# Round one of a two-round graph and state-space kernel: features of two row tiles in one group of VectorE operations, one tile later

## The chip, the cores and the metric

One Trainium2 chip, one core. The time is the device time of one execution in microseconds, and the median of several executions is taken. The profile is one further execution, recorded by the hardware profiler; its span runs from the first to the last instruction.

## The reference

`x` has 4096 rows of 128 features, `adj` is a 4096 x 4096 matrix of 0 and 1. The part that matters here is the graph layer on the normalised x:

```python
e = leaky_relu(x @ a[:F] + (x @ a[F:]).T, 0.2)
U = softmax(where(adj > 0, e, -9e15), axis=1)
prop_u = (0.5 * U) @ x
rowsum = sum(U * 0.5 * U, axis=1)
xi = x * rowsum[:, None]
feat = coe[2] * (prop_u - xi) + (1 - coe[2]) * (x + prop_u - xi)
feat = where(abs(feat) > 1e-6, abs(feat) - 1e-6, 0) * sign(feat)
pu = U @ feat
```

`pu`, `feat` and `h0` are then combined, x is added, and a layer with a gated state-space scan (convolution, softplus, scan over 32 chunks, gate, normalisation, output matrix) follows on the normalised sum.

## The kernel before

The 4096 rows are 32 row tiles of 128. The kernel goes over all of them twice, since `U @ feat` needs every tile's `feat`. **Round one** computes `U @ x` and `rowsum`, and from them each tile's `feat`, which is written over the tile's rows in `xn`. **Round two** computes `U @ feat` and, a few tiles behind, the state-space layer.

Round one runs in 8 supertiles of 4 row tiles (`it` 0 to 3), and each row tile in 4 blocks (`ch` 0 to 3), so 16 blocks b per supertile. The adjacency never takes part as numbers. For supertile G+1, ScalarE (ACT) turns adjacency words into 16-bit `edges` (`sign`, line 1208), TensorE (PE) transposes them (`turn`, line 1550, into one of 4 banks), and VectorE (DVE) compares them with the scores and writes one-byte `code` (`codes`, line 762, two per block). For supertile G, ACT makes `maskA` and DVE makes `maskC` from the code (lines 1271 and 770), two blocks ahead (`LEAD`), in 4 buffers each. PE multiplies both with `Y` (`products`, lines 1609 and 1618): 8 matmuls into `accA`, 8 into `accC`, in one of two banks by the row tile's parity.

There is no scheduler. Every engine runs its own instruction order, which is written out by hand (`supertile` for each of them), and semaphores tie them. Supertile 0 and supertile 7 are written out, and supertiles 1 to 6 are a hardware loop of two. The waits around the change:

- PE, in block b: `products(b)`, then `turn(G+1, b)`. Before the first block of tile T+2, PE waits for ACT's and DVE's reading of tile T's sums (`free_acc`, `acc_read` and `summed`).
- ACT reads tile T's `accA` during block 1 of tile T+1 (`read_acc`).
- DVE, in block b: the mask of block b+2; `codes(G+1, ...)` twice, which wait for PE's turn of block b (`tr_done`); in block 2 also `sum1` of the tile before (line 787), which adds `accC` and counts `summed`. Behind it comes the feature step `feat1` of the tile before that.
- GpSimd (POOL) computes from `ps_sum` the small numbers of a tile and `scaled` and `k_one` (`features`, lines 526 to 545, in a chain of dependent operations). It begins when `summed` says so and counts `scaled_done`. It has two sets of these buffers, by parity, and waits for `feat_done` before it overwrites one. For odd tiles it also adds two finished tiles of `xn` to `featsum` (`feature_sum`, line 551).
- `feat1` waits for `scaled_done`. Its three dependent operations (lines 796 to 798) form the feature, limit it to plus or minus 1e-6, and subtract the two. The last one writes `xn` and counts `feat_done`.

In the last supertile there are no codes to make. Instead ACT and DVE prepare `Y2`, the operand of round two, from finished features (`y2_high`, `y2_low`, lines 1266 and 749, in the order of the table `Y2_AT`). Tiles 30 and 31 have a tail of their own (lines 905 to 931), in which both tiles' limit and subtraction are one operation each.

Of the kernel before, what the change touches and what calls it, by code (L numbers as in the profile page):

```python
# [25 lines left out]
ALU = mybir.AluOpType  # L26
# [5 lines left out]
THRESH = 1e-06  # L32
# [7 lines left out]
def gnn_ffn_kernel(nc, x, adj, h0, a, temp, W_in, conv_w, conv_b, dt_bias, A_log, D, norm_w, W_out, W_lin, b_lin, out):  # L40
    N, F = x.shape
    NT = N // P
    IT = 4
# [19 lines left out]
    with ExitStack() as ctx:  # L63
        def sb(name, shape, dt=F32):
            return ctx.enter_context(nc.sbuf_tensor(name, shape, dt))

        def sem(name):
            return ctx.enter_context(nc.semaphore(name))
# [20 lines left out]
        xn = sb("xn", [P, NT, F])  # L89
# [32 lines left out]
        k_one = sb("k_one", [P, 2, 1])  # L122
# [4 lines left out]
        scaled = sb("scaled", [P, 2, F])  # L127
        fwork = sb("fwork", [P, 2, F])
# [110 lines left out]
        S = {n: sem(n) for n in names}  # L239
# [6 lines left out]
        def wait(eng, name, value):  # L246

            if not isinstance(value, int) or value > 0:
                eng.wait_ge(S[name], value)
# [438 lines left out]
        def _(dve):  # L688
            v = nc.vector
# [54 lines left out]
            def y2_low(t):  # L744

                for side in range(2):
                    dve.wait_ge(S["y2_hi"], 2 * t + side + 1)
                    y = y2_of(t, side)
                    v.scalar_tensor_tensor(out=y[:, 1], in0=xn[:, t, :], scalar=colw[:, side, t, 0:1], in1=y[:, 0].bitcast(F32),
                                           op0=ALU.mult, op1=ALU.subtract).then_inc(S["y2_done"], 1)  # L750
# [6 lines left out]
            def codes(G, par, jt):  # L757

                n = G * NT + jt
                dve.wait_ge(S["tr_done"], n + 1)  # L760
                rows = bass.ds(v.snap(G * 512) if not isinstance(G, int) else G * 512, 512)
                v.scalar_tensor_tensor(  # L762
                    out=code[par][:, :, jt * P:(jt + 1) * P], in0=f1_rows[:, rows].rearrange("p (i r) -> p i r", i=IT),
                    scalar=neg_f2[:, jt:jt + 1], in1=turned(jt),
                    op0=ALU.is_le, op1=ALU.subtract).then_inc(S["coded"], 1)
# [6 lines left out]
            def mask1(G, par, b):  # L772

                if b >= BLOCKS:
                    G, par, b = G + 1, 1 - par, b - BLOCKS
                it, ch = b // NB, b % NB
                dve.wait_ge(S["coded"], G * NT + (NT if it else (ch + 1) * JB))
                mask_c(G * BLOCKS + b, code[par][:, it, ch * JB * P:(ch + 1) * JB * P], b)

            def sum1(T, k):  # L780

                row = v.snap(T) if not isinstance(T, int) else T
                w = roww[:, bass.ds(row, 1), 1:2].rearrange("p a b -> p (a b)")
                dve.wait_ge(S["acc_read"], T + 1)
                wait(dve, "scaled_done", T - 1)
                both = accC[k][:, 0:2 * XC].rearrange("p (a b) -> p a b", a=2)
                v.scalar_tensor_tensor(out=ps_sum[:, k], in0=both, scalar=w, in1=acc_s[:, k], op0=ALU.mult, op1=ALU.add).then_inc(S["summed"], 1)  # L787

            def feat1(T, k):

                row = v.snap(T) if not isinstance(T, int) else T
                mine = xn[:, bass.ds(row, 1), :].rearrange("p a b -> p (a b)")
                wait(dve, "feat_done", T)
                dve.wait_ge(S["scaled_done"], T + 1)
                inside = chain[0] > 0
                link(v.scalar_tensor_tensor(out=fwork[:, 0], in0=mine, scalar=k_one[:, k], in1=scaled[:, k], op0=ALU.mult, op1=ALU.add))
                link(v.tensor_scalar(fwork[:, 1], fwork[:, 0], -THRESH, THRESH, ALU.max, ALU.min))
                v.tensor_tensor(mine, fwork[:, 0], fwork[:, 1], ALU.subtract).then_inc(S["feat_done"], 1)
                if inside:
                    dve.wait_ge(S["feat_done"], T + 1)  # L800
                else:
                    end_chain()

            def supertile(G, par, first=False, last=False):
                for b in range(BLOCKS):
                    it, ch = b // NB, b % NB
                    if not (last and b + LEAD >= BLOCKS):
                        mask1(G, par, b + LEAD)
                    if not last:
                        if b == 0:  # L810

                            wait(dve, "maskA_ready", G * BLOCKS)
                            wait(dve, "spilled", G * IT * 16)
                        if first and b == 0:
                            dve.wait_ge(S["f1_copied"], 8)
                            dve.wait_ge(S["yC_done"], NB)
                            dve.wait_ge(S["yA_done"], NB)
                        for j in range(JH):
                            codes(G + 1, 1 - par, b * JH + j)
                    if ch == 2 and not (first and it < 1):  # L820
                        sum1(G * IT + (it - 1), (it - 1) % 2)
                    if ch == 2 and not (first and it < 2):
                        feat1(G * IT + (it - 2), it % 2)

            chain = [0]

            def step(ins):

                chain[0] += 1
                ins.then_inc(S["vch"], 1)  # L830
                return chain[0]

            def link(ins):

                dve.wait_ge(S["vch"], step(ins))

            def end_chain():
                if chain[0]:
                    dve.wait_ge(S["vch"], chain[0])
                    v.sem_clear(S["vch"])  # L840
                chain[0] = 0
# [29 lines left out]
            def mask2(n, k, j):  # L871

                b = j % NB
                if isinstance(n, int) and n < 2 * NB:

                    T, ch = FIRST[n]
                    dve.wait_ge(S[f"codes_in{T}"], 16)
                    mask_c(n + R1, code0[:, T, ch * JB * P:(ch + 1) * JB * P], b)
                    return
                dve.wait_ge(S[f"codes_in{k}"], code_count(n, k, b))  # L880
                mask_c(n + R1, code0[:, k, b * JB * P:(b + 1) * JB * P], b)

            G = NG - 1
            for b in range(BLOCKS):
                it, ch = b // NB, b % NB
                if b + LEAD < BLOCKS:
                    mask1(G, 1, b + LEAD)
                else:
                    mask2(b + LEAD - BLOCKS, 0, b + LEAD - BLOCKS)
                if ch == (1 if it == IT - 1 else 2):  # L890
                    sum1(G * IT + (it - 1), (it - 1) % 2)
                if ch == 2 and it < IT - 1:
                    feat1(G * IT + (it - 2), it % 2)
                for t in Y2_AT[b]:
                    y2_low(t)

# [26 lines left out]
            for i in range(2):  # L923
                made = step(v.tensor_scalar(fwork[:, i], xn[:, NT - 2 + i, :], k_T[:, i:i + 1], None, ALU.mult))
            dve.wait_ge(S["vch"], made)
            for i in range(2):
                made = step(v.scalar_tensor_tensor(out=fwork[:, i], in0=scaled[:, i], scalar=r_T[:, i:i + 1], in1=fwork[:, i], op0=ALU.mult, op1=ALU.add))
# [268 lines left out]
        def _(act):  # L1196
# [192 lines left out]
            def read_inputs(c, kc):  # L1389
                zdt, _, conv, _ = in_buffers(c)  # L1390
                first, second = in_banks(c)
                own = isinstance(c, int) and c == LAST
                act.wait_ge(S["p_in"], c + 1)
                if not own:
                    wait(act, "dt_ready", c)
                    wait(act, "gate_done", c)
                s.copy(zdt, first[:, 0:DI + NH]).then_inc(S["zcopy"], 1)  # L1397
                wait(act, "conv_pre", c - 1)
                s.copy(hist[:, kc, :, TAPS - 1:], second[:, 0:CB * P].rearrange("p (c w) -> p c w", c=CB))
                if not own:  # L1400
                    wait(act, "conv_ready", c)
                for cb in range(CB):
                    m = s.activation(conv[:, cb], second[:, cb * P:(cb + 1) * P], ACT.Identity, bias=conv_bt[:, cb:cb + 1],  # L1403
                                     scale=conv_wt[:, cb, TAPS - 1:TAPS])
                m.then_inc(S["in_read"], 1)
                if not own:

                    act.wait_ge(S["in_read"], c + 1)
                    wait(act, "conv_pre", c)
                    s.copy(hist[:, 1 - kc, :, 0:TAPS - 1], hist[:, kc, :, P:P + TAPS - 1]).then_inc(S["halo_done"], 1)  # L1410
# [474 lines left out]
```

## Time and profile before

| | |
|---|---|
| median of 3 executions | 808.99 us (808.49 to 809.42) |
| profiled execution | 808.94 us |
| its span | 807.2 us |
| TensorE busy | 756.7 us, 94% |
| VectorE busy | 739.7 us, 92% |
| ScalarE busy | 675.4 us, 84% |
| GpSimd busy | 582.9 us, 72% |
| round one, about | from 47 to 351 us |

A busy time counts the instructions of an engine, not its waiting for semaphores, so the difference from the span is what an engine idles. PE has two lines in the profile: PE for matmuls and PEld for the weight loads that run beside them. Because matmuls are pipelined, a weight load's start tells better than a matmul's when a block began. In the order of time, a start is followed by a duration; a DVE operation's successor can start before its duration is over, so what an operation costs in a row of others is the distance of two starts.

### The profile page before, as it was taken

To read this page: it belongs to the slowest core of one execution; us is meant where nothing else is said; L and a number is where in the kernel's file an instruction comes from. 1 tells how busy PE (TensorE), PEld (TensorE's weight loads), DVE (VectorE), ACT (ScalarE), POOL (GpSimd) and SP (SyncE) were. 2 spreads that over 40 slices of the span, in tenths; PEclk is the share of its full clock that TensorE was granted. 3 is DMA by queue.
4 is the path that set the end of the run, shared out by engine and by line. 5 is a ranking of instruction groups with operands and counts; after the bars stand their busy time and mean duration, and the time that the engine had idled before them with its cause. 6 is when DMAs were issued, how large, how long until landed. Compare 5 with 4: busy or idle time off the path is not lost. (4 is left out here: it accounts for less than half of the span.)

```text
span 807.2 us, 20951 instructions
## 1 busy us (share of the span) xinstructions
PE 756.7 (94%) x6079; PEld 721.4 (89%) x6079; DVE 739.7 (92%) x1934; ACT 675.4 (84%) x1428; POOL 582.9 (72%) x1115
## 2 busy tenths in 40 slices
PE   3689999999999999869999999999999999999976
PEld 1389999999999999868899999999999999999955
DVE  6999999999999999796999999999999999999872
ACT  5989898989989897865888888888898989888761
POOL 5683667776777677856888878788787878788850
PEclk9989999999999999979999999999999999999975
DMA  7689897989889794122111121112121212110000
GB/s 212 191 257 328 267 326 242 336 259 325 273 302 291 258 308 184 29 53 81 56 55 66 44 67 44 65 42 68 42 69 39 68 39 68 46 37 14 5 8 10
DMA packets 97961, 110.43 MB, mean 137 GB/s; under 512 B 6865, under 2 KB 89713, under 8 KB 97905
## 3 DMA queue, kind: packets, MB, share of 16 engines
q1 hardware_dynamic: 97906, 109.78, 41.9%
q8 instruction: 25, 0.41, 0.2%
q14 instruction: 30, 0.25, 0.1%
HBM read 90.87 MB, written 18.89 MB: 136 GB/s over the span
## 5 line engine op out<-in xcount | busy, mean ns | idle before, releaser
L1271 ACT ACTIVATE maskA<-code 128x1024 fp32r<-128x1024 int8 x256 | 269.0, 1053 | 24.9 <-DVE code L762 21.4
L1609 PE MATMUL accA<-Y,maskA 128*128 128x260 f32 (+1 forms) x1792 | 270.6, 294 | 8.9 <-ACT maskA L1271 6.1
L1618 PE MATMUL accC<-Y,maskC 128*128 128x260 f32 (+1 forms) x1792 | 254.6, 285 | 2.6 <-DVE maskC L770 2.6
L1609 PEld LDWEIGHTS accA<-Y,maskA 128*128 128x128 f32 x1792 | 232.6, 191 | 14.4 <-issue 7.8
L1618 PEld LDWEIGHTS accC<-Y,maskC 128*128 128x128 f32 x1792 | 230.6, 191 | 3.6 <-DVE maskC L770 3.6
L770 DVE TENSOR_SCALAR maskC<-code 128x1024 fp32r<-128x1024 int8 x256 | 206.5, 808 | 0.0
L762 DVE SCALAR_TENSOR_TENSOR code<-f_rows,neg_f,ps 128x512 int8<-128x512 int8 (+1 forms) x256 | 177.9, 737 | 0.4 <-DVE neg_f L726 0.2
L1208 ACT ACTIVATE edges<-adj_in 128x1024 int8<-128x1024 f32 x128 | 135.2, 1059 | 1.5 <-DMA adj_in<-in_adj_dram 1.5
L625 POOL TENSOR_TENSOR room_r<-room,room_r 128x256 fp32r<-128x256 f32 x128 | 95.6, 774 | 2.5
L1044 DVE SCALAR_TENSOR_TENSOR room<-room 128x128 f32<-128x128 f32 x279 | 89.5, 342 | 0.0
L1550 PE MATMUL ps<-ident,edges 128*128 128x128 bf16 x512 | 51.2, 224 | 10.2 <-ACT edges L1208 10.2
L1550 PEld LDWEIGHTS ps<-ident,edges 128*128 128x128 bf16 x512 | 30.0, 99 | 20.2 <-ACT edges L1208 11.0
L613 POOL TENSOR_TENSOR room<-room,consts 128x1 f32<-128x1 f32 x32 | 8.7, 272 | 44.2 <-DVE room L1006 44.2
L526 POOL COPY small<-roww 128x2 f32 (+1 forms) x30 | 5.8, 194 | 47.7 <-DVE ps_sum L787 46.2
L1609 PE MATMUL accA<-Y_2a,maskA 128*128 128x256 f32 x256 | 38.0, 290 | 0.0
L1397 ACT COPY room<-ps 128x260 f32<-128x260 f32 x30 | 11.3, 378 | 30.9 <-PE ps L1700 30.9
L1716 PE MATMUL ps<-room 128*128 128x64 f32 x248 | 36.1, 270 | 0.0
L1618 PE MATMUL accC<-Y_2b,maskC 128*128 128x256 f32 x256 | 35.9, 283 | 0.0
L1403 ACT ACTIVATE room<-ps,room 128x128 f32<-128x128 f32 x90 | 35.3, 476 | 0.0
L1716 PEld LDWEIGHTS ps<-room 128*128 128x128 f32 x248 | 34.4, 201 | 0.0
L1452 ACT ACTIVATE room<-room 128x64 f32<-128x64 f32 x124 | 33.2, 343 | 0.0
L1618 PEld LDWEIGHTS accC<-Y_2b,maskC 128*128 128x128 f32 x256 | 32.9, 191 | 0.0
(260 smaller groups left out, 1620.9 us busy)
## 6 DMA issues: line engine op xcount, KB each, us to landing
adj_in<-in_adj_dram SPq DMA_DIRECT2D x128, 512.0 KB, 5.0
edge_codes<-code SPq DMA_DIRECT2D x32, 512.0 KB, 5.5
code<-edge_codes SPq DMA_DIRECT2D x32, 512.0 KB, 3.2
xn<-in_x_dram SPq DMA_DIRECT2D x4, 512.0 KB, 5.6
room<-in_x_dram SPq DMA_DIRECT2D x32, 64.0 KB, 1.8
room<-in_L_gnn_h_dram SPq DMA_DIRECT2D x32, 64.0 KB, 1.9
out_dram<-room SPq DMA_DIRECT2D x32, 64.0 KB, 1.6
room<-in_L_ffn_W_in_dram SPq DMA_DIRECT2D x1, 192.0 KB, 2.5
```

The source lines that it names most:

```text
L625: m = g.tensor_tensor(dam.rearrange("p a h w -> p (a h) w")[:, at], upto.unsqueeze(1).broadcast_to([P, NH // 2, P]), da_parts.rearrange("p ...
L762: v.scalar_tensor_tensor(out=code[par][:, :, jt * P:(jt + 1) * P], in0=f1_rows[:, rows].rearrange("p (i r) -> p i r", i=IT), scalar=neg_f2 ...
L770: v.tensor_scalar(maskC[:, b % MASKS], src, 1.0 - LINK, None, ALU.is_equal).then_inc(S["maskC_ready"], 1)
L1044: ins = v.scalar_tensor_tensor(out=conv[:, cb], in0=hist[:, kc, cb, tap:tap + P], scalar=conv_wt[:, cb, tap:tap + 1], in1=conv[:, cb], op0 ...
L1208: s.activation(pair, adj_in[:, h % 4].rearrange("p i (e w) -> p i e w", e=JH), ACT.Relu, bias=FREE, scale=HUGE).then_inc(S["signed"], 1)
L1271: s.activation(maskA[:, b % MASKS], src, ACT.Relu, bias=1.0 - LINK, scale=-1.0).then_inc(S["maskA_ready"], 1)
L1403: m = s.activation(conv[:, cb], second[:, cb * P:(cb + 1) * P], ACT.Identity, bias=conv_bt[:, cb:cb + 1], scale=conv_wt[:, cb, TAPS - 1:TAPS])
L1452: last = s.activation(xdtd[:, h * HD:(h + 1) * HD], xdt[:, h * HD:(h + 1) * HD], ACT.Copy, scale=expD[:, h, P - 1:P])
L1550: m = t_.matmul(ps[b % TRB][:, it * P:(it + 1) * P], edges[:, b % EDGE_SLOTS, it], ident2[:], start=True, stop=True)
L1609: t_.matmul(accA[k][:, 0:2 * cols], maskA[:, b % MASKS, l * P:(l + 1) * P], y2_of(jt, 0) if cols == F else Y[:, jt, 0, :, 0:cols], start=j ...
L1618: m = t_.matmul(accC[k][:, 0:2 * cols], maskC[:, b % MASKS, l * P:(l + 1) * P], y2_of(jt, 1) if cols == F else Y[:, jt, 1, :, 0:cols], sta ...
L1716: t_.matmul(ps[0][:, h * HD:(h + 1) * HD], mix_of(c)[:, h], xdt[:, h * HD:(h + 1) * HD], start=False, stop=h == (kb + 1) * P // HD - 1)
```

## The change

A new function treats tiles T and T+1 (T even) together. Two operations form the features, one per tile, without a wait between them. One operation limits both, one subtracts both and counts `feat_done` by 2. It stands where the second tile's `feat1` stood, so the first tile's feature comes one tile later. The limited values go to `scaled`, as in the tail of tiles 30 and 31. Tiles 28 and 29 keep their single `feat1`.

```diff
+            def feat_pair(T):
+
+                row = v.snap(T) if not isinstance(T, int) else T
+                both = xn[:, bass.ds(row, 2), :]
+                wait(dve, "feat_done", T)
+                for i in range(2):
+                    dve.wait_ge(S["scaled_done"], T + 1 + i)
+                    mine = xn[:, bass.ds(v.snap(T + i) if not isinstance(T, int) else T + i, 1), :].rearrange("p a b -> p (a b)")
+                    made = step(v.scalar_tensor_tensor(out=fwork[:, i], in0=mine, scalar=k_one[:, i], in1=scaled[:, i], op0=ALU.mult, op1=ALU.add))
+                dve.wait_ge(S["vch"], made)
+                link(v.tensor_scalar(scaled[:], fwork[:], -THRESH, THRESH, ALU.max, ALU.min))
+                v.tensor_tensor(both, fwork[:], scaled[:], ALU.subtract).then_inc(S["feat_done"], 2)
+                end_chain()
...
-                    if ch == 2 and not (first and it < 2):
-                        feat1(G * IT + (it - 2), it % 2)
+                    if ch == 2 and it % 2 == 1 and not (first and it < 2):
+                        feat_pair(G * IT + (it - 3))
...
-                if ch == 2 and it < IT - 1:
-                    feat1(G * IT + (it - 2), it % 2)
+                if ch == 2 and it == 1:
+                    feat_pair(G * IT - 2)
+                if ch == 2 and it == 2:
+                    feat1(G * IT, 0)
```

DVE's order in block 2 of row tile 2 (it = 2 of supertile 0, from the `sum1` of tile 1 on). Line 787 is `sum1`, 796 to 798 are `feat1`, 840 clears the counter of dependent operations, 770 is the mask and 762 the codes. Before:

```order
L787 SCALAR_TENSOR_TENSOR ps_sum<-accC,roww,acc_s 128x260 [waits acc_read]
L796 SCALAR_TENSOR_TENSOR fwork<-xn,k_one,scaled 128x128 [waits scaled_done]
L797 TENSOR_SCALAR fwork<-fwork 128x128 [waits vch]
L798 TENSOR_TENSOR xn<-fwork 128x128 [waits vch]
L840 ISA [waits vch]
L770 TENSOR_SCALAR maskC<-code 128x1024 [waits mm_done,coded]
L762 SCALAR_TENSOR_TENSOR code<-f_rows,neg_f,ps 128x4x128 [waits tr_done] x2
```

And now, at the same place:

```order
L787 SCALAR_TENSOR_TENSOR ps_sum<-accC,roww,acc_s 128x260 [waits acc_read]
L770 TENSOR_SCALAR maskC<-code 128x1024 [waits mm_done,coded]
L762 SCALAR_TENSOR_TENSOR code<-f_rows,neg_f,ps 128x4x128 [waits tr_done] x2
L770 TENSOR_SCALAR maskC<-code 128x1024 [waits mm_done,coded]
L762 SCALAR_TENSOR_TENSOR code<-f_rows,neg_f,ps 128x4x128 [waits tr_done] x2
```

The feature step is gone from behind this `sum1`, and the next mask follows it at once. The same holds for every `sum1` of an odd tile in the loop.

DVE's order one tile later (it = 3, from the `sum1` of tile 2 on). In the new numbering, 812 to 815 are `feat_pair` and 854 is the clearing. Before:

```order
L787 SCALAR_TENSOR_TENSOR ps_sum<-accC,roww,acc_s 128x260 [waits scaled_done,acc_read]
L796 SCALAR_TENSOR_TENSOR fwork<-xn,k_one,scaled 128x128 [waits scaled_done,feat_done]
L797 TENSOR_SCALAR fwork<-fwork 128x128 [waits vch]
L798 TENSOR_TENSOR xn<-fwork 128x128 [waits vch]
L840 ISA [waits vch]
L770 TENSOR_SCALAR maskC<-code 128x1024 [waits mm_done,coded]
```

And now:

```order
L787 SCALAR_TENSOR_TENSOR ps_sum<-accC,roww,acc_s 128x260 [waits scaled_done,acc_read]
L812 SCALAR_TENSOR_TENSOR fwork<-xn,k_one,scaled 128x128 [waits scaled_done] x2
L814 TENSOR_SCALAR scaled<-fwork 128x256 [waits vch]
L815 TENSOR_TENSOR xn<-fwork,scaled 128x256 [waits vch]
L854 ISA [waits vch]
L770 TENSOR_SCALAR maskC<-code 128x1024 [waits mm_done,coded]
```

The step of one tile has become that of two, with four operations for six. The order of PE, ACT, POOL and the DMA queue is the same in both kernels.

## Rows read from the trace of the kernel before

**Rows 1.** The page: busy time and share of the span of each engine.
```profile
PE 756.7 (94%) x6079; PEld 721.4 (89%) x6079; DVE 739.7 (92%) x1934; ACT 675.4 (84%) x1428; POOL 582.9 (72%) x1115
```

**Rows 2.** Table by stretch: length, then busy us of PE, PEld, DVE, ACT, POOL.
```profile
200.24:209.35 9.11, 9.11 (x84) 8.90 (x84) 9.04 (x17) 6.31 (x9) 5.95 (x14) 1.00 0.68 224
209.35:218.28 8.93, 8.89 (x81) 8.55 (x80) 8.86 (x18) 8.93 (x12) 6.77 (x15) 1.00 0.88 289
```

**Rows 3.** Order of time, 200 to 219 us: start, duration, engine, line, operation.
```profile
200.24 0.48 DVE L787 SCALAR_TENSOR_TENSOR ps_sum<-accC,roww,acc_s 128x260 f32<-128x260 f32 x1
200.64 0.34 DVE L796 SCALAR_TENSOR_TENSOR fwork<-xn,k_one,scaled 128x128 f32<-128x128 f32 x1
...
201.50 0.68 DVE L770 TENSOR_SCALAR maskC<-code 128x1024 fp32r<-128x1024 int8 x1
...
202.10 1.39 DVE L762 SCALAR_TENSOR_TENSOR code<-f_rows,neg_f,ps 128x512 int8<-128x512 int8 x2
...
203.42 0.68 DVE L770 TENSOR_SCALAR maskC<-code 128x1024 fp32r<-128x1024 int8 x1
...
207.16 0.40 POOL L544 TENSOR_TENSOR scaled<-featw,small 128x128 f32<-128x128 f32 x1
207.25 0.86 DVE L770 TENSOR_SCALAR maskC<-code 128x1024 fp32r<-128x1024 int8 x1
...
207.29 0.40 PE L1550 MATMUL ps<-ident,edges 128*128 128x128 bf16 x4
...
208.03 1.39 DVE L762 SCALAR_TENSOR_TENSOR code<-f_rows,neg_f,ps 128x512 int8<-128x512 int8 x2
...
209.35 0.48 DVE L787 SCALAR_TENSOR_TENSOR ps_sum<-accC,roww,acc_s 128x260 f32<-128x260 f32 x1
...
209.90 1.03 PEld L1609 LDWEIGHTS accA<-Y,maskA 128*128 128x128 f32 x8 [0.18 <-issue]
...
218.83 1.03 PEld L1609 LDWEIGHTS accA<-Y,maskA 128*128 128x128 f32 x8
```

**Rows 4.** Order of time in supertile 0, 79 to 93 us, around tiles 1 and 2.
```profile
79.27 1.41 DVE L762 SCALAR_TENSOR_TENSOR code<-f_rows,neg_f,ps 128x512 int8<-128x512 f32 x2 [0.20 <-PE ps L1550]
...
81.04 0.40 PE L1550 MATMUL ps<-ident,edges 128*128 128x128 bf16 x4
...
81.48 1.41 DVE L762 SCALAR_TENSOR_TENSOR code<-f_rows,neg_f,ps 128x512 int8<-128x512 f32 x2
...
83.25 0.40 PE L1550 MATMUL ps<-ident,edges 128*128 128x128 bf16 x4
83.43 1.02 PEld L1609 LDWEIGHTS accA<-Y,maskA 128*128 128x128 f32 x8
...
91.95 0.48 DVE L787 SCALAR_TENSOR_TENSOR ps_sum<-accC,roww,acc_s 128x260 f32<-128x260 f32 x1
...
92.67 0.42 PEld L1609 LDWEIGHTS accA<-Y,maskA 128*128 128x128 f32 x3 [0.37 <-issue]
```

**Rows 5.** Order of time on DVE in the tail, tiles 30 and 31.
```profile
356.00 0.61 DVE L927 SCALAR_TENSOR_TENSOR fwork<-scaled,row_out,fwork 128x128 f32<-128x128 f32 x2
356.65 0.29 DVE L929 TENSOR_SCALAR scaled<-fwork 128x256 f32<-128x256 f32 x1
356.97 0.43 DVE L930 TENSOR_TENSOR xn<-fwork,scaled 128x256 f32<-128x256 f32 x1
357.32 2.54 DVE L749 SCALAR_TENSOR_TENSOR Y<-xn,colw,Y 128x128 fp32r<-128x128 f32 x8
```

**Rows 6.** Order of time on PEld: the gate behind tile 26's `sum1`.
```profile
309.08 1.02 PEld L1609 LDWEIGHTS accA<-Y,maskA 128*128 128x128 f32 x8
```

**Rows 7.** Who waited for whom, 308 to 360 us: us in total, times, longest.
```profile
DVE fwork L796 <- POOLq L457: 6.6, 3, 2.9
...
PE accC L1618 <- DVE maskC L770: 2.3, 3, 1.3
POOL small L526 <- POOL row_out L545: 1.5, 3, 0.7
```

## The prediction

> **What bounds the kernel now.** I read the page's first part, then a table of busy time by stretch, then the order of time around one row tile. The page has TensorE (PE) busy for 94% of the span and VectorE (DVE) for 92% [rows 1]. The table by stretch has both at 99 to 100% in a tile of round one [rows 2]. So shares do not say who waits. The order of time does [rows 3]. PE's first weight load of a tile's first block (call it the gate) comes at 209.90 and at 218.83. The first is 0.07 us behind the end of a `sum1` on DVE (209.35 + 0.48 = 209.83). A block of PE takes 2.21 us (two turns without a wait between them, 81.04 and 83.25, [rows 4]), so four take 8.83 us, but these gates are 8.93 us apart, and those from 92.67 to 309.08, over 24 tiles, 9.02 us on average [rows 4, 6]. PE therefore waits about 0.2 us per tile for DVE, and DVE never rests: **DVE sets the pace by the last step of a short loop**. The loop is this: `codes(b)` waits for PE's turn of block b, `sum1` stands behind the codes of block 2, and PE's gate of the tile after next waits for `sum1`.
>
> How far may DVE run ahead? Hardly at all. In block 2 the codes start at 208.03, and PE's turn of the same block ended at 207.29 + 0.40 = 207.69 [rows 3]: 0.34 us of room. One tile of the trace has no feature step behind its `sum1`, the first one, and shows what happens with less work on DVE: codes start at 79.27 with idle time put down to PE's turn, then at 81.48, one PE block later and 0.04 us behind the end of the turn of 81.04 [rows 4]. There DVE runs at PE's pace, its spare time is lost, and the gate comes at 83.43, 0.18 us behind the turn, which is PE's unhindered distance.
>
> **The change part by part.** For tiles 0 to 27 the six feature instructions of two tiles become four, 14 times. They all stand behind the `sum1` of an even tile; the `sum1` of an odd tile is followed by the next mask.
>
> DVE's work. Going by starts, a mask holds DVE for 0.60 us (201.50 to 202.10), two codes for 1.32 (202.10 to 203.42), a `sum1` for 0.40 (200.24 to 200.64) and a single feature step for 0.86 (200.64 to 201.50) [rows 3]. A tile is 4 x 1.92 + 0.40 = 8.08 us without a feature and 8.94 with one; the interval of 8.93 from 209.35 to 218.28 [rows 2] agrees. The pair's price is to be had from the tail of round one, where tiles 30 and 31 are treated in the same way [rows 5]: 0.65 us for two SCALAR_TENSOR_TENSOR (356.00 to 356.65), 0.32 for the limit over 256 elements, 0.35 for the subtraction, 1.32 us in all. So DVE is saved 2 x 0.86 - 1.32 = 0.40 us per pair. That is 14 x 0.40 = 5.6 us if all of it were on the path.
>
> It is not, because the work is now uneven: 8.08 us in one tile, 9.40 in the next. **Light interval** (from the gate behind an odd tile's `sum1` to that behind an even tile's): DVE needs 8.08 us, PE 8.83. DVE is held by the turns, as in [rows 4], and the gates are 8.83 apart. **Heavy interval**: at its start DVE has no lead. Its codes start 1.95 us ahead of the gate (81.48 and 83.43, [rows 4]). 9.40 us later the next codes of block 2 start, `sum1` ends 1.32 + 0.48 = 1.80 us after that, and the gate opens 0.07 us later [rows 3] or 0.24 (91.95 + 0.48 = 92.43, gate 92.67, [rows 4]); both distances come back in runs of tiles, and I take the middle, 0.15. That makes 9.40 - 1.95 + 1.80 + 0.15 = 9.40 us.
>
> To it comes one collision. In the interval from 200.24 the mask at 207.25 took 0.86 us instead of 0.68 while POOL's `scaled` operation ran from 207.16 [rows 3]; the next interval has none, and 9.11 against 8.93 us is this difference [rows 2]. It falls behind the `sum1` of an even tile, which is where the heavy interval lies. Its price is bounded from below by 0 (the four-tile pattern of starts moves by 0.46 us and may miss it) and from above by two such collisions, 0.36; I take 0.18, since the work of POOL that starts with an even tile's `sum1` stays the same. The heavy interval is then 9.58 us. A test of the method: the same sum with a feature of 0.86, the late gate of 0.24 and 0.18 gives 8.94 - 1.95 + 1.80 + 0.24 + 0.18 = 9.21; the trace has 92.67 - 83.43 = 9.24 [rows 4], after just such a light interval.
>
> The Trainium skill, page "SBUF — State Buffer", section "Who interferes with whom", calls this an exclusive lock between VectorE and GpSimd, and adds that a VectorE operation with two SBUF inputs takes part in it too. By that, the pair's 256-element subtraction may collide as well, and the sum would go to the upper bound; the row of 356.97 shows it undisturbed, with no such neighbour named there.
>
> Sum. A light and a heavy interval take 8.83 + 9.58 = 18.41 us; now 24 intervals from 92.67 to 309.08 are 12 pairs of 18.03. 12 x 0.38 = +4.6 us. The interval from 83.43 to 92.67 loses the feature step behind tile 1's `sum1` and becomes light: 8.83 - 9.24 = -0.4. In the last supertile there are no codes, and what paces it is POOL: DVE waits 6.6 us in three waits for its `scaled`, and POOL goes from one tile's operations to the next with 0.7 us or less between [rows 7]. This chain starts at tile 26's `sum1`, which will end about 0.15 us ahead of its gate instead of 0.06: -0.1. The feature of tile 26, for which DVE waits there, moves one tile on; POOL hides what this saves. The pair that takes its place adds 0.46 us to a tile in which PE already waits for maskC (2.3 us in three waits, [rows 7]); I cost it at nothing, since POOL's chain is longer, and at 0.5 if it were not. `feature_sum` on POOL asks for both features of an older pair and finds them done. Round two gets nothing new. **+4.6 - 0.4 - 0.1 = +4.1 us.** The profiled execution took 808.94, 0.05 below the median of the runs: 813.0.
>
> **The rivals.** Two tenths of a per cent, 1.6 us, is about what a measurement can tell here.
>
> *DVE keeps its lead* (0.07). If the time saved in a light interval could be carried over, the pair of tiles would be DVE's 18.03 - 0.40 = 17.63, or PE's floor of 17.66. That is 12 x 0.37 + 0.4 = 4.8 us less: 804.1, faster. It decides at the codes of block 2: they would have to start more than 0.5 us ahead of where the turn now lets them. For it speaks that two instructions in six vanish; against it the rows of the first tile.
>
> The Trainium skill, page "VectorE: DVE Perf Modes", section on the TRN2 errata, has a fixed cost of 58 cycles at 0.96 GHz for each instruction that reads SBUF. As an estimate from that page, 28 fewer instructions are 1.7 us, which gives 807.2 if DVE is the path throughout. The rows give more for the merging and deny that it is the path throughout.
>
> *Two collisions in a heavy interval* (0.17). 9.76 instead of 9.58, 12 x 0.18 = 2.2 us more: 815.2. For it: masks now start 0.46 us later against the fourteen operations that POOL issues for a tile, any of which can stand in the way. With the late gate of 0.24 throughout as well it is 816.3.
>
> *No collision* (0.11). 2.2 us less than forecast: 810.8; with the early gate of 0.07 throughout, 809.9, which counts as no change. I give half of this case to either.
>
> *The change does not reach the end* (0.04), since something I have not seen, DMA or ScalarE, paces the tiles and refills what moves: 808.9. The gates' distance of 0.07 to 0.24 us from `sum1` speaks against it.
>
> *POOL is late for the pair* (0.01): the odd tile's `scaled` is now needed at the second instruction. The single step needed it at the same place, so the price is small.
>
> **How the numbers follow.** My forecast has 0.60. Slower: 0.60 + 0.17 + 0.06 + 0.01 = 0.84. Within 0.2%: 0.05 + 0.04 = 0.09. Faster: 0.07. The range leaves out the faster rival, the case of no effect and the outer ends: 810.3 to 815.8.
>
> **What would show it.** In the profile after, intervals between gates should alternate at 8.8 and 9.5 to 9.6 us. DVE should show idle time, or masks and codes drawn out, behind PE's turns in tiles that have no pair. The pair's operations should take 0.34, 0.34, 0.29 and 0.43 us. DVE's busy time for features should fall by some 5 us and the span grow by 4. Intervals of 8.83 throughout would make it wrong, and so would codes that start before the turn of their block has ended by my reading.

## The result, and the profile after

The changed kernel takes 813.39 us in the median of 5 executions (810.08 to 814.42), the kernel before 808.49 in its 5 of the same comparison. The ratio is 1.0063, with a 95% interval of 1.0041 to 1.0085: **slower by 0.6%, some 5 us**. A second series of the same kernel, told of below, has 813.46 against 809.05, ratio 1.0059 [1.0036, 1.0083].

The page of the kernel after, busy time by engine, answers to [rows 1]:

```profile
PE 750.9 (93%) x6079; PEld 716.5 (89%) x6079; DVE 739.8 (92%) x1906; ACT 675.5 (84%) x1428; POOL 595.0 (74%) x1115
```

DVE has 28 instructions fewer, and the durations of its feature instructions add up to 4.7 us less. Yet its busy time has not moved, since it counts time that two instructions cover only once: in an unhindered row each starts a little before the last has ended (a mask of 0.68 us is followed after 0.60), and where DVE is held this overlap is gone. The groups of DVE by shape show the part of the holding that the profile calls idle. The columns are line, engine, operation and shapes, count, busy us and mean ns, and then idle us before them with what ended it. Before:

```profile
L762 DVE SCALAR_TENSOR_TENSOR code<-f_rows,neg_f,ps 128x512 int8<-128x512 int8 x192 | 133.9, 736 | 0.0
```

After:

```profile
L762 DVE SCALAR_TENSOR_TENSOR code<-f_rows,neg_f,ps 128x512 int8<-128x512 int8 x192 | 134.3, 740 | 5.8 <-PE ps L1566 5.8
L812 DVE SCALAR_TENSOR_TENSOR fwork<-xn,k_one,scaled 128x128 f32<-128x128 f32 x28 | 8.6, 344 | 2.8 <-POOLq L457 2.8
L815 DVE TENSOR_TENSOR xn<-fwork,scaled 128x256 f32 x12 | 5.1, 425 | 1.2
L814 DVE TENSOR_SCALAR scaled<-fwork 128x256 f32<-128x256 f32 x14 | 4.1, 295 | 0.5
```

Before, the codes never idled; now DVE idles 5.8 us ahead of them, all of it put down to PE's turn (line 1566 in the new numbering). More of the wait lies inside instructions: the codes of 220.15 below start 0.88 us behind their mask of 219.27, where 0.60 is the unhindered distance, and the profile calls 0.20 of this 0.28 idle.

Table by stretch of the kernel after, the intervals between `sum1` of tiles 14, 15 and 16 (length, then busy us of PE, PEld, DVE, ACT, POOL). It answers to [rows 2]:

```profile
203.03:212.71 9.68, 9.67 (x90) 9.23 (x88) 9.54 (x18) 6.38 (x9) 6.91 (x16) 1.00 0.66 212
212.71:221.47 8.76, 8.18 (x73) 8.06 (x74) 8.33 (x14) 8.76 (x12) 6.86 (x14) 1.00 0.88 288
```

What was 9.11 and 8.93 is now 9.68 and 8.76. Order of time of the kernel after, the same stretch, answers to [rows 3]. Lines 1566 and 1625 are PE's turn and first product.

```profile
203.03 0.48 DVE L787 SCALAR_TENSOR_TENSOR ps_sum<-accC,roww,acc_s 128x260 f32<-128x260 f32 x1
203.43 0.61 DVE L812 SCALAR_TENSOR_TENSOR fwork<-xn,k_one,scaled 128x128 f32<-128x128 f32 x2
203.66 1.02 PEld L1625 LDWEIGHTS accA<-Y,maskA 128*128 128x128 f32 x8
204.07 0.29 DVE L814 TENSOR_SCALAR scaled<-fwork 128x256 f32<-128x256 f32 x1
204.07 0.33 POOL L526 COPY small<-roww 128x2 f32 x1 [0.67 <-DVE ps_sum L787]
204.47 0.43 DVE L815 TENSOR_TENSOR xn<-fwork,scaled 128x256 f32 x1
204.81 0.69 DVE L770 TENSOR_SCALAR maskC<-code 128x1024 fp32r<-128x1024 int8 x1
...
210.46 0.46 POOL L543 TENSOR_TENSOR featw<-featw,num 128x128 f32<-128x128 f32 x1
210.57 0.91 DVE L770 TENSOR_SCALAR maskC<-code 128x1024 fp32r<-128x1024 int8 x1
...
211.40 1.39 DVE L762 SCALAR_TENSOR_TENSOR code<-f_rows,neg_f,ps 128x512 int8<-128x512 int8 x2
...
212.71 0.47 DVE L787 SCALAR_TENSOR_TENSOR ps_sum<-accC,roww,acc_s 128x260 f32<-128x260 f32 x1
...
213.26 1.02 PEld L1625 LDWEIGHTS accA<-Y,maskA 128*128 128x128 f32 x8 [0.73 <-issue]
...
219.27 0.68 DVE L770 TENSOR_SCALAR maskC<-code 128x1024 fp32r<-128x1024 int8 x1
219.72 0.40 PE L1566 MATMUL ps<-ident,edges 128*128 128x128 bf16 x4
...
220.15 1.41 DVE L762 SCALAR_TENSOR_TENSOR code<-f_rows,neg_f,ps 128x512 int8<-128x512 int8 x2 [0.20 <-PE ps L1566]
...
221.47 0.48 DVE L787 SCALAR_TENSOR_TENSOR ps_sum<-accC,roww,acc_s 128x260 f32<-128x260 f32 x1
...
222.10 1.02 PEld L1625 LDWEIGHTS accA<-Y,maskA 128*128 128x128 f32 x8
```

The gates are at 203.66, 213.26 and 222.10: 9.60 us for the heavy interval, in which PE waits 0.7 us for `sum1`, and 8.84 for the light one. At the end of the light one, the codes (220.15) start 0.03 us behind the end of PE's turn (219.72 + 0.40). This is the picture of [rows 4], now in every second tile. Over the 12 pairs from tile 2 to tile 26, light intervals are 8.82 to 8.93 us (mean 8.87), heavy ones 9.59 to 9.68 (9.64), 18.50 together instead of 18.03.

By the end of round one (the gate behind tile 31's `sum1`), the kernel after is 5.3 us behind: 356.52 against 351.23. Yet the span of its first profile is only 1.2 us longer, 808.4. The last update of x1 in round two begins 5.1 us later than before (769.9 against 764.8), so the 3.9 us come back in the drain behind it. The tables of this stretch show the clock (the third number from the right). Before:

```profile
764.00:780.00 16.00, 12.87 (x68) 11.29 (x68) 14.65 (x54) 9.57 (x34) 8.56 (x18) 0.77 0.02 6
780.00:808.00 28.00, 17.49 (x70) 14.59 (x68) 8.10 (x23) 7.24 (x28) 6.53 (x13) 0.62 0.03 10
```

After:

```profile
764.00:780.00 16.00, 12.46 (x94) 11.25 (x93) 12.99 (x44) 12.82 (x45) 10.20 (x23) 1.00 0.02 6
780.00:808.00 28.00, 18.09 (x87) 14.86 (x86) 13.46 (x42) 8.72 (x34) 9.42 (x18) 0.70 0.03 10
```

Here the granted clock of TensorE was 0.77 and 0.62 of its upper level (2.4 GHz) before, and 1.00 and 0.70 after. The stretches are fixed in time while the drain begins 5.1 us later, so a part of the first difference is only the shift. The rest, 0.70 against 0.62, is a difference between two executions, as the next section shows.

### The profile page after: what moved, and what is told of

It is laid out like the page before. It is cut to its first block and busy times, and to the rows that moved or that the text cites. A ratio compares the mean times of both kernels' runs of the same rounds, so it can differ in the third digit from the quotient of the medians.

```text
span 808.4 us, 20909 instructions
## 1 busy us (share of the span) xinstructions
PE 750.9 (93%) x6079; PEld 716.5 (89%) x6079; DVE 739.8 (92%) x1906; ACT 675.5 (84%) x1428; POOL 595.0 (74%) x1115
## 5 line engine op out<-in xcount | busy, mean ns | idle before, releaser
L526 POOL COPY small<-roww 128x2 f32 (+1 forms) x30 | 11.2, 373 | 41.4 <-DVE ps_sum L787 39.9
```

## The experiments

**The same kernel again.**

> The changed kernel once more, for a second profile and more executions. The tile intervals should repeat to 0.02 us (8.87 and 9.64), the last tiles of round one should stand 5.1 to 5.5 us behind the kernel before, and the median should be 4 to 5.5 us above it. The first profile had a span only 1.2 us longer; if that lay in the clock of the drain at the end (mean granted clock 0.979 against 0.970), it does not repeat.

Measured: 813.46 us (811.94 to 815.68) against 809.05, ratio 1.0059 [1.0036, 1.0083]. All intervals repeat within 0.03 us, tile 31's gate is at 356.57, and the span is 812.2, 5.0 above the profile before. Its last x1 update begins at 771.1. Its drain had this clock:

```profile
764.00:780.00 16.00, 12.94 (x97) 11.66 (x95) 12.99 (x47) 12.13 (x42) 10.12 (x24) 1.00 0.01 5
780.00:808.00 28.00, 20.74 (x87) 17.77 (x86) 14.75 (x42) 9.05 (x36) 9.71 (x17) 0.62 0.02 6
```

It took 41 us from that update to the end, the first profile 38.5, the kernel before 42.4. The 5 us of round one repeat; what the drain gives back does not.

**The delay without the merging.**

```diff
-                        feat_pair(G * IT + (it - 3))
+                        feat1(G * IT + (it - 3), 0)
+                        feat1(G * IT + (it - 2), 1)
```

(and likewise in the last supertile)

> Both features of a pair stand one tile later, as in the change, but as two single steps of three operations each: the delay without the merging. Theory A (in the tile without features DVE is held by PE's turns and its spare time is lost; the tile with both features then pays all of it at the gate): the heavy interval grows by 2 x 0.86 - 1.32 = 0.40 us over that of the change, from 9.64 to about 10.04, the light one stays at 8.87; 12 x 0.40 = 4.8 us more than the change, so about 818 us, 1.2% above the kernel before. Theory B (the place does not matter, the merged operations over 256 elements are what costs, by their collisions with POOL): the old operations bring the old time back, about 808.5.

Measured: 820.88 us against 809.23, ratio 1.0141 [1.0121, 1.0161]. Order of time, the gates of tiles 14, 15 and 16:

```profile
206.81 1.02 PEld L1627 LDWEIGHTS accA<-Y,maskA 128*128 128x128 f32 x8
...
216.94 1.02 PEld L1627 LDWEIGHTS accA<-Y,maskA 128*128 128x128 f32 x8 [1.11 <-issue]
```

The heavy interval is 10.13 to 10.20 us from tile 7 on, the light one stays at 8.83 to 8.92. So the very operations of the kernel before, at another place, cost 11.6 us; theory B falls. The heavy interval grew by 0.53 instead of 0.40: the two single steps hold DVE for 2.14 us (206.58 to 208.72) instead of 1.72, where the pair took 1.38, and the long mask of the change is missing (0.76 - 0.23 = 0.53). The merging by itself gains some 7 us against this kernel; the delay takes more.

**`sum1` ahead of the mask and codes of its block**, on the change and on the kernel before.

```diff
+                    if ch == 2 and not (first and it < 1):
+                        sum1(G * IT + (it - 1), (it - 1) % 2)
                     if not (last and b + LEAD >= BLOCKS):
                         mask1(G, par, b + LEAD)
...
-                    if ch == 2 and not (first and it < 1):
-                        sum1(G * IT + (it - 1), (it - 1) % 2)
```

> The change, with sum1 moved to the head of block 2, ahead of the mask and the codes of that block (supertiles 0 to 6), so that PE's gate asks for it 1.9 us and more before it is due. Theory A: the gate no longer waits, the late work of a heavy tile is taken up by the room between sum1 and the gate, and DVE catches up in the light tile. A pair of intervals falls from 18.50 us to what DVE needs, 2 x 8.08 + 1.32 = 17.5 plus a collision or two, or PE's floor of 17.66, whichever is more: about 17.8. 12 x 0.7 = 8 us less than the change, so about 805, and below the kernel before. Theory B: DVE's work is the same and so is the time, about 813.

> The kernel before with sum1 at the head of block 2 in the same way. Theory A: here DVE has no time to spare in any tile (8.94 us of work each, PE 8.83), so an earlier sum1 cannot help: a pair stays at 2 x 8.94 + 0.18 = 18.06, time 808.5 within 1.5 us. If the wait at the gate cost by itself (its 0.07 to 0.24 us of latency, 24 times), it would fall by 2 to 5 us.

Measured: on the change 806.70 us against 809.23, ratio 0.9968 [0.9952, 0.9983]; on the kernel before 806.86, ratio 0.9974 [0.9955, 0.9992]. With the change, the loss is gone. Of its 6.7 us, 2.4 are what the same edit gives the kernel before, for a reason of its own (below); the other 4.3 are the time that the change had lost. The pair then neither costs nor gains: 806.70 and 806.86. The `sum1` of tiles 14, 15 and 16, on DVE:

```profile
196.85 0.48 DVE L787 SCALAR_TENSOR_TENSOR ps_sum<-accC,roww,acc_s 128x260 f32<-128x260 f32 x1
206.72 0.48 DVE L787 SCALAR_TENSOR_TENSOR ps_sum<-accC,roww,acc_s 128x260 f32<-128x260 f32 x1
214.94 0.48 DVE L787 SCALAR_TENSOR_TENSOR ps_sum<-accC,roww,acc_s 128x260 f32<-128x260 f32 x1
```

DVE now runs at its own pace, 9.87 + 8.22 = 18.09 us per pair. It no longer waits in light tiles (8.22 is below PE's 8.83), but 18.09 is 0.3 more than I expected, and no less than the 18.03 of the kernel before. DVE's bare work is 17.48. These lines of the heavy interval show what stretches it:

```profile
199.17 0.77 DVE L812 SCALAR_TENSOR_TENSOR fwork<-xn,k_one,scaled 128x128 f32<-128x128 f32 x2
...
200.74 0.69 DVE L770 TENSOR_SCALAR maskC<-code 128x1024 fp32r<-128x1024 int8 x1
...
204.47 0.46 POOL L543 TENSOR_TENSOR featw<-featw,num 128x128 f32<-128x128 f32 x1
204.57 0.91 DVE L770 TENSOR_SCALAR maskC<-code 128x1024 fp32r<-128x1024 int8 x1
```

The pair holds DVE for 1.57 us (199.17 to 200.74) instead of 1.32, one mask is 0.23 longer, and another, beside POOL's `featsum` operation, 0.14: 17.48 + 0.25 + 0.37 = 18.10.

On the kernel before, the intervals of `sum1` are unchanged (9.10 and 8.93), and yet it is 2.4 us faster, which my expectation put outside its bound. The gain is a single one: `sum1` stands 1.9 us earlier in the order, DVE is no longer held in the first tile, which has no feature step (8.07 instead of 8.75 us), and later tiles add hundredths. So POOL's chain for the last supertile starts at 306.21 instead of 309.19, and tile 31's gate comes 2.5 us earlier.

**PE's turn ahead of its block's products**, on both.

```diff
+                    if not last:
+                        turn(G + 1, b)
                     if ch == 0 and not (first and it < 2):
 
                         free_acc(G * IT + (it - 2))
                     products(G * BLOCKS + b, it % 2, b, ch, XC, 1 if first and it == 0 else None)
-                    if not last:
-                        turn(G + 1, b)
```

> The change, with PE's turn of a block ahead of the products of that block and ahead of the wait at the gate, instead of behind them: DVE's codes may start one PE block (2.2 us) earlier. sum1 stays where it was. Theory A: DVE keeps the time of the light tile as a lead and spends it in the heavy one: pair of intervals about 17.7 to 17.9 us, about 805 us. If DVE is not held by the turns (A wrong in that step), nothing changes: 813. Theory B: 813.

> The kernel before with PE's turn ahead of the products of its block. DVE has 8.94 us of work in each tile, more than PE's 8.83, so a lead gives it nothing to spend: pair of intervals 18.0 to 18.1 us. PE may get ahead once by some 1.5 to 2.5 us, as with the earlier sum1 (2.4 us faster): about 806.5 to 807.5. With the change on top the same edit gave 809.7, with pairs of 18.26 us on DVE; if that excess over 17.5 is collisions with POOL brought by the pair, here it should be absent.

Measured: on the change 809.72 us against 809.23, ratio 1.0009 [0.9991, 1.0027]; on the kernel before 808.06 against 809.05, ratio 0.9988 [0.9970, 1.0006]. DVE's hold by the turns is real: with it gone the change gets 3.7 us back (the kernel before, 1.0), and its light intervals fall to 8.22. But the pair is 10.04 + 8.22 = 18.26 us. Order of time at the feature step of this kernel:

```profile
218.01 0.47 DVE L787 SCALAR_TENSOR_TENSOR ps_sum<-accC,roww,acc_s 128x260 f32<-128x260 f32 x1
218.41 0.34 DVE L812 SCALAR_TENSOR_TENSOR fwork<-xn,k_one,scaled 128x128 f32<-128x128 f32 x1
218.49 0.30 POOL L545 COPY row_out<-small 128x4 f32 x1 [0.17 <-POOL scaled L544]
219.02 0.35 DVE L812 SCALAR_TENSOR_TENSOR fwork<-xn,k_one,scaled 128x128 f32<-128x128 f32 x1 [0.27 <-POOLq L457]
```

This is the rival to which I gave 0.01: once the light tile is short, POOL's work for the odd tile (over 8 us) is not ready when the pair asks for it. The second operation starts 0.61 us behind the first instead of 0.27. The kernel before shows no such thing with the same edit; its pair stays at 18.05.

**The pair split**: the even tile's operation one tile earlier.

```diff
+            def feat_open(T):
+
+                wait(dve, "feat_done", T)
+                dve.wait_ge(S["scaled_done"], T + 1)
...
+                step(v.scalar_tensor_tensor(out=fwork[:, 0], in0=mine, scalar=k_one[:, 0], in1=scaled[:, 0], op0=ALU.mult, op1=ALU.add))
+                end_chain()
...
+                    if ch == 2 and it % 2 == 0 and not (first and it < 2):
+                        feat_open(G * IT + (it - 2))
```

> The change with its first operation (the feature of the even tile, one SCALAR_TENSOR_TENSOR) done one tile earlier, behind the sum1 of the odd tile; the other three stay. It evens the two tiles out a little: about 0.3 us go from the heavy to the light one. Theory A (time is lost by unevenness, since DVE is held by PE's turns in the light tile and cannot work ahead): the light interval stays at 8.87, the heavy one falls from 9.64 to about 9.35; 12 x 0.3 = 3.5 us less than the change, about 809.5 to 810. Theory B (the merged operations cost by themselves): no change from 813.4, rather a bit more, for one more clearing of the counter per pair.

Measured: 816.78 us (814.03 to 819.01) against 809.05, ratio 1.0100 [1.0075, 1.0126]: not faster than the change, against my expectation. Its tile 26 gate is where the change has it (314.60 and 314.55). The reason is in the order of time:

```profile
221.50 0.19 POOL L545 COPY row_out<-small 128x4 f32 x1 [0.17 <-POOL scaled L544]
...
221.91 0.35 DVE L819 SCALAR_TENSOR_TENSOR fwork<-xn,k_one,scaled 128x128 f32<-128x128 f32 x1 [0.32 <-POOLq L457]
```

In the change, the first of the two operations fills just the time in which POOL finishes. Moved away, it leaves a wait of the same length. Of the further 3.3 us above the change, 1.2 lie in the last supertile (tile 31's gate at 357.74). Another 1.3 lie between tile 31's `sum1` and the last x1 update (416.7 us, 415.4 in the second profile of the change), where the granted clock was 0.91 from 370 to 390 us instead of 0.99. One profile does not show whether that belongs to the kernel.

**POOL shortened**, on the change, and then with the pair split. Both kernels leave out the part for rows without neighbours (the product of `col_mean` with their flag and its addition), which for these data adds zero.

```diff
-                link(g.tensor_tensor(featw[:, 0], col_mean[:], n["zn"].broadcast_to([P, F]), ALU.mult))
-                link(g.tensor_tensor(featw[:, 1], featw[:, 0], num[:, 0:F], ALU.add))
-                link(g.tensor_tensor(scaled[:, k], featw[:, 1], n["r"].broadcast_to([P, F]), ALU.mult))
+                link(g.tensor_tensor(scaled[:, k], num[:, 0:F], n["r"].broadcast_to([P, F]), ALU.mult))
```

> The change with two of POOL's fourteen operations per tile left out: the product of col_mean with the flag for an empty row and its addition to the sums (for these data the flag is 0 throughout). The mask at the end of the heavy interval then finds another operation of POOL, or none, beside it. Collision theory: in the change this mask takes 0.91 us instead of 0.68 since it starts while the addition runs; without it the heavy interval falls from 9.64 to 9.4 or 9.5, 12 x 0.15 to 0.24 = 2 to 3 us; in the last supertile POOL's chain of four tiles gets 4 x 0.95 us shorter, up to 3.8 us more: 807 to 810. If the long mask has another cause, the heavy interval stays and only the last supertile gains: 809.5 to 811.

> The split pair (first operation one tile earlier) with the two operations of POOL left out as in pool_short, so that POOL's result for the odd tile is there in time. In split_pair the second feature waited for POOL (0.3 us, starting 0.22 us behind POOL's last operation) and nothing was won. Theory A: with POOL in time, the heavy interval falls by about 0.3 us against pool_short, from 9.67 to about 9.35 (give or take one collision of 0.2), 12 x 0.3 = 3.5 us: about 807 against 810.3. If unevenness were not what costs, it would stay at 810.

Measured: shortened alone, 810.32 us against 809.05, ratio 1.0017 [1.0000, 1.0034]; with the split, 807.40 against 809.00, ratio 0.9986 [0.9973, 0.9998]. The first one's heavy interval did not fall, it is 9.60 to 9.70. The long mask is no longer at the end of the interval, but at its beginning, beside another wide operation of POOL:

```profile
207.44 0.67 POOL L529 TENSOR_TENSOR num<-ps_sum 128x130 f32<-128x130 f32 x1
207.75 0.91 DVE L768 TENSOR_SCALAR maskC<-code 128x1024 fp32r<-128x1024 int8 x1
```

So the long mask moved with POOL's operations, as a collision does, but it did not go away with the one that was removed. What this kernel gains over the change lies in the last supertile. With the split on top, POOL is in time, and now the evening out works as theory A has it. Gates of tiles 14, 15 and 16 of this kernel:

```profile
201.94 1.02 PEld L1634 LDWEIGHTS accA<-Y,maskA 128*128 128x128 f32 x8
...
211.28 1.03 PEld L1634 LDWEIGHTS accA<-Y,maskA 128*128 128x128 f32 x8 [0.47 <-issue]
...
220.13 1.02 PEld L1634 LDWEIGHTS accA<-Y,maskA 128*128 128x128 f32 x8
```

9.34 us (9.42 in the other tiles) against 9.62 (9.70), and 8.85: from tile 2 to 26, the pair falls from 18.52 to 18.24 us, 12 x 0.28 = 3.4 us; the medians differ by 2.9.

**Candidates for a faster kernel**: both early, then the pair one block later, then all three.

```diff
-                    if ch == 2 and it % 2 == 1 and not (first and it < 2):
+                    if ch == 3 and it % 2 == 1 and not (first and it < 2):
                         feat_pair(G * IT + (it - 3))
```

> The change with both edits that loosen PE and DVE: sum1 at the head of block 2, and PE's turn ahead of its block's products. Neither engine should then wait for the other more than once in a few tiles; the pace is DVE's own work. With sum1 early alone that was 18.09 us per pair, with collisions with POOL (24 long masks in 24 tiles, 0.2 us each) in it. If that is DVE's own pace, it stays at 18.1 and the time at 806 to 807. If the remaining waits of sum_early_after on turns (room 0.02 us in one tile in four) cost as well, it falls to 17.9 and 804.

> sum1 at the head of block 2, and the pair one block later, behind the codes of block 3, so that POOL's ten small operations meet other masks. A candidate for a kernel faster than both. DVE's bare work is 17.47 us per pair, PE's 17.66. Without long masks: 17.7 per pair, 18.09 - 17.7 = 0.4, 12 x 0.4 = 5 us less than sum_early_after, 802. If just as many collide as before: 806.7. POOL waits for the pair before it may write the next numbers; it comes there 4.6 us after sum1, the pair is done by then.

> sum1 at the head of block 2, PE's turn ahead of its products, and the pair behind the codes of block 3: the two candidates together. With sum1 early and the pair in block 3, DVE's pair of intervals was 17.8 us undisturbed, and PE waited for sum1 in some tiles only (intervals of 8.97 instead of 8.83). If the earlier turn takes these waits away too, the pair comes to 17.75 to 17.8 throughout, 0.15 to 0.2 less than the mean of 17.95 there, 12 x 0.15 = 2 us: 803.5. If DVE's own pace with its long masks is the limit in both, it stays at 805.5 to 806.5.

Measured: both early 806.45 us against 809.00, ratio 0.9958 [0.9940, 0.9977]; `sum1` early with the pair in block 3, 805.51, ratio 0.9966 [0.9951, 0.9981]; all three, **802.56 us against 809.01, ratio 0.9933 [0.9911, 0.9955]**. The first has 9.86 + 8.21 = 18.07 us per pair on DVE, as with `sum1` early alone: DVE's own pace is the limit. The second lies between its two forecasts of 802 and 806.7, with DVE at 17.91 us per pair in the mean. In the last one DVE has this, the `sum1` of tiles 15, 16 and 17 and the pair between:

```profile
204.00 0.47 DVE L787 SCALAR_TENSOR_TENSOR ps_sum<-accC,roww,acc_s 128x260 f32<-128x260 f32 x1
...
212.22 0.47 DVE L787 SCALAR_TENSOR_TENSOR ps_sum<-accC,roww,acc_s 128x260 f32<-128x260 f32 x1
...
216.46 0.60 DVE L812 SCALAR_TENSOR_TENSOR fwork<-xn,k_one,scaled 128x128 f32<-128x128 f32 x2
217.09 0.29 DVE L814 TENSOR_SCALAR scaled<-fwork 128x256 f32<-128x256 f32 x1
217.49 0.42 DVE L815 TENSOR_TENSOR xn<-fwork,scaled 128x256 f32 x1
...
221.81 0.48 DVE L787 SCALAR_TENSOR_TENSOR ps_sum<-accC,roww,acc_s 128x260 f32<-128x260 f32 x1
```

8.22 + 9.59 = 17.81 us per pair, with POOL's numbers long there when the pair comes; over all 12 pairs the mean is 17.91, as in the second kernel, and PE is nearly the slower one (17.66). Tile 31's gate is at 345.92, 5.3 us ahead of the kernel before.

How much of this is the merging? The fair comparison is with `sum1` early on the kernel before. Against it (806.86 us; 18.03 us per pair) the second candidate takes 274.42 us from tile 0's `sum1` to tile 31's instead of 275.79, 1.4 us less. The medians differ by as much, but the intervals of the two ratios overlap. The third takes 274.33 us there, hardly less than the second. These profiles do not explain why its median is 3 us lower than the second's, and both early edits without the merging were never run together. So of the 6.4 us, the traces show some 1.4 for the merging at its later place; how the rest divides is open.

## Why the prediction was right

The direction, the mechanism and the size held: 813.0 forecast, 813.39 measured. That the two agree to 0.4 us is luck in part. The trace's own terms add up to 5.6 - 0.3 - 0.2 = 5.1 us where the forecast had 4.1, and the medians differ by 4.9 and 4.4.

- *DVE sets the pace by the loop of codes, `sum1` and gate.* Held: in the change all gates but the undisturbed ones stand 0.07 to 0.24 us behind `sum1`; taking the loop apart at either of its ends (`sum1` early, turn early) recovers 6.7 and 3.7 us on the change, against 2.4 and 1.0 on the kernel before, whose intervals of `sum1` stay as they were, since DVE has nothing to spare there.
- *Saved time is lost in light tiles.* Held: at the end of every light interval the room at the codes of block 2 is 0.04 us, idle time ahead of the codes is 5.8 us where it was none. (The 0.34 us of room that I gave for the kernel before was that of one tile; its tiles have 0.06 to 0.41.)
- *The pair costs 1.32 us.* It took 1.38 (203.43 to 204.81): the limit holds DVE for 0.40 instead of 0.32. A collision with POOL's copy of 204.07 does not explain it: the distance is 0.40 to 0.42 in all 14 pairs, also where the copy was over long before (starts at 130.04 and 130.44, the copy ended at 130.05), and 0.40 in the last kernel above, where other operations of POOL are near. Why the tail has 0.32 is open. By the rule of the Trainium skill, page "SBUF — State Buffer", section "Who interferes with whom", the subtraction could have waited for POOL; no run shows that it did. The row of 356.97, which I had called undisturbed with no neighbour named, did have one: an operation of POOL over 128x30 from 356.86 to 357.10.
- *Light interval 8.83.* Measured 8.87: in half of the tiles PE still waits by 0.08 us, since the late gate's distance of 0.24 is more than the 0.15 by which `sum1` is early. The light interval that I had taken as a model was of the other kind.
- *Heavy interval 9.58.* Measured 9.64; the one collision is there, 0.23 us instead of 0.18.
- *12 pairs give +4.6.* They give 18.50 against 18.03, 5.6 us. The two steps above are the difference.
- *-0.4 for the interval behind tile 1.* It is 8.92 instead of 9.24: -0.3.
- *The last supertile hides its extra 0.46 us, and -0.1.* Held: the lag is 5.5 us at tile 26 and 5.3 at tile 31.
- *DVE's busy time for features falls by some 5 us.* Held, 4.7. Only in one sign did the first profile mislead: I had said that the span would grow by 4. It grew by 1.2, with a faster clock in the drain, and by 5.0 in the second.
- The rival "POOL is late" was dismissed too lightly. In the change POOL is in time by less than 0.1 us: its last operation before the pair ends at 203.41 (203.22 + 0.19), DVE in the other two kernels follows such an end by 0.22 us, and the second operation starts at about 203.70.

## What to carry to other kernels

Merging two steps of an engine that sets the pace saves its time only if the engine may run ahead during the lighter stretch. Look for the nearest thing that it waits for (here a transposition of the same block, 0.06 to 0.41 us away) before counting the saving, and for what stands behind the merged step in the order (here the small operation on which the next gate waits). Give it room first, by moving the released work earlier: that took away the 5 us that the pair had cost here. A gain from the merging itself, some 1.4 us in the traces, showed only when the pair had also been moved to where its inputs were long there. And run each such edit on the kernel without the change too: without the 2.4 us that `sum1` early gives the kernel before, one would credit the merging with a gain that it does not have.

## What the runs showed of the hardware

A mask of DVE takes 0.68 us alone. If it starts while POOL is in an operation over 128 elements or more, what counts is how long that operation still runs. With 0.31 us left it is 0.18 longer (207.25, kernel before), with 0.36 left 0.23 (210.57, the change), with 0.56 left 0.43 (once, `sum1` early on the change), always the time left less 0.13. With 0.11 left, nothing is added, nor where POOL's operation began only 0.01 us before the mask (then POOL's takes 0.95 instead of 0.40). The case with 0.11, in the kernel before:

```profile
216.07 0.40 POOL L542 TENSOR_TENSOR featw<-col_mean,small 128x128 f32<-128x128 f32 x1
216.36 0.69 DVE L770 TENSOR_SCALAR maskC<-code 128x1024 fp32r<-128x1024 int8 x1
```

So 24 of the 96 masks between the gates behind tiles 2 and 26 start beside such an operation in the kernel before, but only 12 are long: 0.2 us in the distance of two starts decides. In the change 12 of 96 are long too. Beside POOL's operations on one element (52 of the 84 short masks of the change) masks stay at 0.68 or 0.69. It is POOL that is drawn out there, 0.79 instead of 0.25 us for the operation at 206.66, although it began 0.07 us ahead of the mask. A wide operation that starts behind the mask is drawn out too (0.73 instead of 0.40 us for `scaled` at 211.00 in the kernel after). The Trainium skill, page "SBUF — State Buffer", section "Who interferes with whom", says that whichever starts first keeps the shared ports and the other waits; the trace agrees for wide operations, up to the 0.13 us at their end, and not by these start times for the small one of 206.66. Freed of the waits on PE, DVE collides twice as often (23 of 96 masks with `sum1` early), which is a part of why the saving of 0.4 us per pair did not show there.

PE's first load behind a `sum1` follows it by 0.07 us in some tiles and by 0.24 in others, in runs of four tiles that return with the loop of two supertiles; why is open.
